# Two graph-network layers on one core: transposing the next feed-forward chunk, and the masks, without TensorE

## The chip, the cores and the metric

The kernel runs on one core of a Trainium2 chip. The metric is the device time of one execution in microseconds (us), as the median of several runs. A core has five engines that run side by side and wait for one another by semaphores: TensorE (PE; its weight load is PEld), VectorE (DVE), ScalarE (ACT), GpSimd (POOL) and SyncE (SP), which here only issues DMAs.

## The reference, cut to what matters

64 graphs of 128 nodes with 256 features each (`x`, float32) and a 128x128 adjacency matrix per graph (`adj`) go through two layers.

```
# layer 0: attention with 8 heads of 32, then a feed-forward net
normed  = layernorm(x)
q, k, v = normed @ Wq + bq, normed @ Wk + bk, normed @ Wv + bv
weights = softmax(q k^T / sqrt(32) + (2 adj - 1)) * (0.25 + 0.75 adj), rows brought to sum 1
x = x + (weights @ v) @ Wo + bo
x = x + gelu(layernorm(x) @ Wf1 + bf1) @ Wf2 + bf2       # 256 -> 1024 -> 256
# layer 1: two graph attentions, 8 heads and then 1
attn = graph_attention(layernorm(x), bias=adj, W1, ...) + x
out  = graph_attention(layernorm(attn), bias=adj, W2, ...) + attn
```

## The kernel before, in words

The graphs are worked in 16 chunks of 4 (`NC` = 16, `G` = 4), and `x_all` holds all of `x` in SBUF. Four stages run one after the other, each a loop over the 16 chunks: attention (`a_step`), feed-forward (`b_step`), first graph attention (`c1_step`), second graph attention (`c2_step`). Every engine has its own program, with functions of these names; the order within it is written out by hand, and semaphores tie them together. The diff and the prediction also count layernorms: `c = i + CB` is the one that the feed-forward stage of chunk `i` reads.

Big products are done in float32r as three matmuls, high times high, high times low, low times high. So each input exists as a high and a low part: `xh`, `xl` for the normalised input, `gh`, `gl` for the gelu's output.

A layernorm goes so: VectorE takes statistics (`stats`, L284) and aggregates them (`aggr`, L289); GpSimd computes `rstd` (`rstd_of`, L868 and L870); VectorE (L295, in the feed-forward stage) or ScalarE (L1024) writes the normalised rows `xn`; TensorE transposes them, 8 transposes of 128x128, into two PSUM banks (`ln_turn`, L1260); ScalarE copies these to `xh` (`ln_hi`, L978); VectorE subtracts to get `xl` (`ln_lo`, L301).

The feed-forward stage of chunk `i`. TensorE makes the first product in 8 slices `f` of 128 hidden features (`wide`, L1235 to L1237, 6 matmuls each, banks `f % 4`). For each slice ScalarE computes the gelu twice, to `gf` and to `gh` (L1088, L1089), and VectorE subtracts to get `gl` (L546). `gf` has two buffers: ScalarE writes that of slice `f` only when `gl` of slice `f - 2` is done. Then TensorE transposes the next chunk's `xn` (`ln_turn`), and makes the second product graph by graph, 24 matmuls each (L1461 to L1463); for every slice it waits for that slice's `gl`. VectorE adds each result to `x_all` (L579). Among its subtractions VectorE prepares the next chunk: two statistics behind subtraction 0 and two behind 1, the aggregates behind 2, the normalisation behind 4; `ln_lo` behind 7. GpSimd adds the bias to the next chunk's rows once they are normalised (`add_bias`, L849). In the chunk before the last, TensorE computes constants of the next stage behind the third graph (`setup_constants`, L1266 and L1281), which wait for the `xl` of the last chunk.

The masks. In the attention and first graph-attention stages SyncE loads a chunk's adjacency matrices to `adj_in` (two buffers) in one DMA (L768, L804). TensorE transposes them to bank `F[0]` (`adj_turn`, L1328). In attention ScalarE makes an exponential of it (`ft`, L983) and VectorE combines the two (L449); in graph attention ScalarE's exponential of it is kept in `gt_all` (L1105). The load of a later chunk is gated by these transposes.

In the attention stage TensorE also transposes the exponentials of the logits (`a_turn`, L1347), which VectorE scales (`a_pt_out`, L461). In the first graph-attention stage TensorE makes ratios (`ratios`, L1509) that VectorE scales (`c_scale`, L630).

Of the kernel before, what the change touches and what calls it, by code (L numbers as in the profile page):

```python
# [22 lines left out]
F32 = mybir.dt.float32  # L23
# [5 lines left out]
P = 128  # L29
# [25 lines left out]
def build(nc, x, adj, wq, bq, wk, bk, wv, bv, wo, bo, g1, b1, g2, b2, wf1, bf1, wf2, bf2,  # L55
# [4 lines left out]

    ctx = ExitStack()
    with ctx:
# [48 lines left out]
        REGION = 58 * 1024  # L111
# [28 lines left out]
        ft_sb = [o(f"ft{r}", [P, G, P]) for r in range(2)]  # L140
        e_sb = o("e_sb", [P, 2 * H, P])
# [22 lines left out]
        marks = o("marks", [P, 8])  # L164

# [61 lines left out]
        ln_nm = sem("ln_nm")  # L227
        adj_t = sem("adj_t")
        sp_gates = sem("sp_gates")
# [40 lines left out]

        def hb_view(par):
            return hb[par][:].rearrange("p (g h c) -> p g h c", g=G, h=H)
# [9 lines left out]
        def _(dve):  # L282
# [19 lines left out]


# [141 lines left out]

            def a_ft_out(i, par):
                dve.wait_ge(a_et, i + 1)
                f = ft_sb[par][:].rearrange("p g n -> p (g n)")
                dve.scalar_tensor_tensor(out=f, in0=F[0][:], scalar=1.0 / 3.0, in1=f, op0=ALU.add, op1=ALU.mult).then_inc(a_ft, 1)  # L449
# [42 lines left out]
            def a_step(i, half, par):  # L492
                first, tail = (isinstance(i, int) and i == n for n in (0, NC))
                for pp in range(2):
                    s, sp = i * G + (2 * pp - G), i * 2 + (pp - 2)
                    back = not (isinstance(s, int) and s < 2)
                    old = not (isinstance(s, int) and s < 3)
                    if not first:
                        a_max(sp, 0)
                    if pp == 0 and not first:  # L500
                        ln_lo(i + CA)
                    if not first:
                        a_max(sp, 1)
# [24 lines left out]
                    if pp == 0 and not tail:  # L528
                        aggr(i + CA + 1)
            chunks(dve, a_step)  # L530
# [8 lines left out]
            def b_step(i, half, par):  # L539
                final = isinstance(i, int) and i == NC - 1  # L540
                nxt = 0 if final else i + 1
                for f in range(FT):
                    if f == 2:
                        dve.wait_ge(ln_st, (i + CB + 2) * G)
# [4 lines left out]
                    if f < 2:  # L549
                        stats(i + CB + 1, nxt, 2 * f)  # L550
                        stats(i + CB + 1, nxt, 2 * f + 1)
                    if f == 2:
                        aggr(i + CB + 1)
                    if final and f == 2:
                        setup_constants()
                    if f == 4:
                        normalise(i + CB + 1, nxt)
                    if final and f == 5:
                        dve.wait_ge(b_x, 3 * G)
                        dve.wait_ge(ln_mv, (CC + 1) * G)  # L560
                        for g in range(G):
                            stats(CC + 1, 1, g)
# [193 lines left out]
        def _(sp):  # L756
# [10 lines left out]
            def load_adj(i, half, par):  # L767
                sp.dma_start(adj_in[par][:], adj[bass.ds(i * G, G)].rearrange("g p n -> p g n")).then_inc(adj_ld[par], 16)  # L768

            def load_a(i, half, par):  # L770
# [6 lines left out]
                load_adj(i, half, par)  # L777
# [9 lines left out]
            def a_step(i, half, par):  # L787
                if not (isinstance(i, int) and i == NC - 1):
                    load_a(i + 1, half + par, 1 - par)
                if par == 1 and not (isinstance(i, int) and i == 1):  # L790
# [11 lines left out]
            def load_c(i, par, first):  # L802
                gate(adj_t, i + (first - CB - 1))
                sp.dma_start(adj_in[par][:], adj[bass.ds(i * G, G)].rearrange("g p n -> p g n")).then_inc(adj_ld[par], 16)  # L804
# [5 lines left out]
            def c2_step(i, half, par):  # L810
                if not (isinstance(i, int) and i == 0):

                    gate(d_y, i * G)
                    sp.dma_start(out[bass.ds(i * G - G, G)].rearrange("g p d -> p g d"), y_sb[1 - par][:]).then_inc(y_out[1 - par], 16)
            gate(a_x, NG)
            for w, name in ((w1, "w1"), (w2, "w2")):
                sp.dma_start(stage[name][:], kp(w)).then_inc(w_l1, 16)
            for n, a in enumerate((as1, ad1, as2, ad2)):
                sp.dma_start(a_bc[n][:], a.rearrange("h k -> (h k)").partition_broadcast(P)).then_inc(w_l1, 16)
            load_c(0, 0, CC)  # L820
# [137 lines left out]
        def _(act):  # L958
# [21 lines left out]

            def a_adj(i, par):
                act.wait_ge(adj_t, i + 1)
                act.activation(ft_sb[par][:].rearrange("p g n -> p (g n)"), F[0][:], ACT.Exp,  # L983
# [97 lines left out]
            def b_step(i, half, par):  # L1081
# [8 lines left out]
                ln_hi(i + CB + 1)  # L1090
# [5 lines left out]
                if isinstance(i, int) and i == NC - 1:  # L1096
                    act.activation(warm[:], zero_g[:], ACT.Exp)
                    normalise(0, CC, range(G))
                    gt_out(0)
# [3 lines left out]
            def gt_out(i):  # L1103
                act.wait_ge(adj_t, i + NC + 1)
                act.activation(gt_all[:, bass.ds(i * W4, W4)], F[0][:], ACT.Exp).then_inc(c_gt, 1)  # L1105

            def c1_step(i, half, par):
# [7 lines left out]
                if back:  # L1115
                    gt_out(i)
# [76 lines left out]
            act.wait_ge(a_x, NG)  # L1193
            chunks(act, b_step)
# [37 lines left out]
        def _(pe):  # L1232
# [76 lines left out]
            def a_proj(i, n):  # L1309

                wait_for(pe, *(((ln_xl, (i + CA) * KT + 2)), (a_ft, i + 1), (a_qkev, i * 4 + 1), (a_qkev, i * 4 + 2))[n])
# [9 lines left out]

            def adj_turn(c, half, par, first):

                before = {CA: 0, CC: NC // 2}[first]
                pe.wait_ge(adj_ld[par], (half + 1 + before) * 16)
                pe.wait_ge(ln_xl, c * KT + 1)
                for g in range(G):
                    r = pe.transpose(F[0][:, g * P:(g + 1) * P], adj_in[par][:, g, :], ident[:])  # L1328
                r.then_inc(adj_t, 1)
# [46 lines left out]
            def a_step(i, half, par):  # L1376
                first, tail = (isinstance(i, int) and i == n for n in (0, NC))
                for pp in range(2):
# [19 lines left out]
                    if not tail:  # L1398
                        if pp == 0:
                            adj_turn(i + CA, half, par, CA)  # L1400
# [45 lines left out]
            def b_step(i, half, par):  # L1446
# [6 lines left out]
                ln_turn(i + CB + 1)  # L1453
                hi, lo = whl["wf2"]
                for g in range(G):
# [11 lines left out]
                    if isinstance(i, int) and i == NC - 1:  # L1467
                        if g == 0:
                            c_st(0, 0, 0)
                            c_st(0, 1, 0)  # L1470
                            adj_turn(CC, 0, 0, CC)
# [63 lines left out]
            def c1_step(i, half, par):  # L1535
# [11 lines left out]
                if back:  # L1547
                    adj_turn(i + CC, half, par, CC)
                    ratios(i - 1, 1 - par, 1)
                pe.wait_ge(c_gt, i + 1)  # L1550
# [125 lines left out]
```

## Time and profile before

| | |
|---|---|
| median of 3 runs | 1127.02 us (1126.33 to 1127.25) |
| the profiled execution | 1125.41 us, span 1123.6 us |
| busy TensorE, VectorE, ScalarE, GpSimd | 1070.8, 772.3, 713.8, 408.0 us |
| granted TensorE clock | 0.989 of full speed |

The span is the time from the first to the last recorded instruction; the execution takes a little more. Attention lasts to about 417 us of the span, the feed-forward stage to about 790 us, the first graph attention to about 1000 us. A row of a timeline gives the start in us, the duration in us (for a row `xN` that of N instructions together), the engine, the line, the operation, what it writes and reads, and in brackets how long the engine had been idle and for whom. The next instruction on an engine may start before the last one's recorded end.

### The profile page before, as it was taken

The page shows a single profiled execution, that of the slowest core. Times are in us where ns is not written, and L with a number is a line of the kernel's source. Part 1 is how long each engine was busy: PE and PEld are TensorE (multiplying, and loading weights), DVE is VectorE, ACT ScalarE, POOL GpSimd, SP SyncE. Part 2 cuts the span into 40 slices and gives each one's busy share as a digit, 9 for nine tenths or more (in the row PEclk, how much of TensorE's full clock was granted, in tenths as well). Part 3 has the DMA queues.
Part 4 walks back from the last instruction along what each step waited for, and adds up shares of the span by engine and source line. Part 5 has one row for each costly group of instructions (what it writes and reads, how often), then busy time and mean ns, then how long its engine had stood idle before and what let it go on. Part 6 is the DMA issues. An engine that isn't in the chain of part 4 may idle for free.

```text
span 1123.6 us, 38526 instructions
## 1 busy us (share of the span) xinstructions
PE 1070.8 (95%) x16172; PEld 945.3 (84%) x16172; DVE 772.3 (69%) x1889; ACT 713.8 (64%) x1718; POOL 408.0 (36%) x628
## 2 busy tenths in 40 slices
PE   5999999999999989999999999999999999979997
PEld 5888888888888868899889998998888888868886
DVE  4577777677776767754455445545788888859996
ACT  2777767777677755543555345536688788857774
POOL 3431121121121113332223222322387777775662
PEclk9999999999999999999999999999999999989999
DMA  7001101111100001000000000000010001002122
GB/s 225 30 30 58 32 31 31 30 31 59 30 13 2 3 27 33 1 1 1 1 1 1 1 1 1 1 1 11 11 33 22 23 23 33 3 3 73 61 76 94
DMA packets 41804, 32.10 MB, mean 29 GB/s; under 512 B 5280, under 2 KB 41376, under 8 KB 41632
## 3 DMA queue, kind: packets, MB, share of 16 engines
q1 hardware_dynamic: 37312, 29.36, 8.2%
q8 instruction: 128, 2.10, 0.8%
q10 hardware_dynamic: 4320, 0.28, 0.3%
q14 instruction: 44, 0.36, 0.1%
HBM read 21.25 MB, written 8.39 MB: 26 GB/s over the span
## 4 chain that ended last, share of the span: by engine, by line
PE 71%; POOL 11%; issue 9%; DVE 6%; ACT 2%; ACTq 1%; POOLq 0%; DVEq 0%
PE BK L1235 8%; PE BK L1237 8%; PE BK L1236 8%; PE BK L1373 6%; PE BK L1461 5%; PE BK L1462 5%; PE BK L1463 5%; PE BK L1347 5%; PE BK L1359 4%; PE BK L1340 3%; POOL x_all L938 3%; POOL x_all L849 3%; PE BK L1260 3%; POOL atc L930 2%; POOL rstd L870 1%
## 5 line engine op out<-in xcount | busy, mean ns | idle before, releaser
L1088 ACT ACTIVATE gf<-BK,bcol 128x512 f32<-128x512 f32 x128 | 88.1, 689 | 182.7 <-PE BK L1237 167.4
L868 POOL TENSOR_TENSOR ve<-mv,eps_l 128x4 f32<-128x4 f32 x64 | 15.4, 240 | 438.7 <-DVE mv L289 405.8
L1004 ACT ACTIVATE e_sb<-BK,nmx 128x128 f32<-128x128 f32 x512 | 141.5, 403 | 28.3 <-DVE nmx L455 28.3
L1461 PE MATMUL BK<-wf_hi,gh 128*128 128x256 f32 x512 | 143.5, 280 | 0.0
L1462 PE MATMUL BK<-wf_hi,gl 128*128 128x256 f32 x512 | 141.8, 277 | 0.0
L1463 PE MATMUL BK<-wf_lo,gh 128*128 128x256 f32 x512 | 141.7, 277 | 0.0
L546 DVE TENSOR_TENSOR gl<-gf,gh 128x512 fp32r<-128x512 f32 x128 | 93.4, 731 | 62.9 <-ACT gh L1089 61.1
L461 DVE TENSOR_TENSOR pt_sb<-BK,ft 128x512 f32<-128x512 f32 x128 | 85.2, 686 | 70.1 <-PE BK L1347 68.5
L1024 ACT ACTIVATE xn<-x_all,neg_mr,rstd 128x256 f32<-128x256 f32 x188 | 103.8, 611 | 5.2 <-POOL neg_mr L877 4.8
L1237 PE MATMUL BK<-xh,wf_lo 128*128 128x512 f32 x256 | 100.8, 394 | 0.0
L1236 PE MATMUL BK<-xl,wf_hi 128*128 128x512 f32 x256 | 100.6, 393 | 0.0
L1235 PE MATMUL BK<-xh,wf_hi 128*128 128x512 f32 x256 | 99.9, 390 | 0.5 <-DVE x_all L477 0.5
L579 DVE TENSOR_TENSOR x_all<-BK,x_all 128x256 f32<-128x256 f32 x64 | 27.1, 423 | 105.3 <-PE BK L1463 105.3
L455 DVE TENSOR_REDUCE nmx<-BK 128x8 f32<-128x1024 f32 x64 | 76.7, 1219 | 32.9 <-PE BK L1340 32.9
L1462 PEld LDWEIGHTS BK<-wf_hi,gl 128*128 128x128 f32 x512 | 96.3, 188 | 0.0
L1463 PEld LDWEIGHTS BK<-wf_lo,gh 128*128 128x128 f32 x512 | 96.2, 188 | 0.0
L1461 PEld LDWEIGHTS BK<-wf_hi,gh 128*128 128x128 f32 x512 | 96.1, 188 | 0.0
L284 DVE BATCH_NORM_STATS2 st<-x_all 128x6 f32<-128x256 f32 x256 | 92.1, 411 | 4.6 <-DMA x_all<-in_x_dram 4.1
L630 DVE SCALAR_TENSOR_TENSOR pp<-BK,gt_all 128x512 f32<-128x512 f32 x128 | 81.9, 682 | 16.6 <-PE BK L1509 16.6
L849 POOL TENSOR_TENSOR x_all<-x_all,bo_bc 128x256 f32<-128x256 f32 x64 | 44.6, 730 | 133.2 <-ACT xn L1024 118.6
L849 POOL TENSOR_TENSOR x_all<-x_all,c_bc 128x256 f32<-128x256 f32 x128 | 89.9, 733 | 4.0 <-ACT xn L1024 2.6
L1089 ACT ACTIVATE gh<-BK,bcol 128x512 fp32r<-128x512 f32 x128 | 87.0, 680 | 0.0
(204 smaller groups left out, 2869.7 us busy)
## 6 DMA issues: line engine op xcount, KB each, us to landing
x_all<-in_x_dram SPq DMA_DIRECT2D x16, 512.0 KB, 4.1
adj_in<-in_adj_dram SPq DMA_DIRECT2D x32, 256.0 KB, 2.9
out_dram<-y SPq DMA_DIRECT2D x16, 512.0 KB, 3.0
s_wf<-in_L_gnn_Wf_dram SPq DMA_DIRECT2D x2, 1024.0 KB, 9.9
s_w<-in_L_gnn_W_dram SPq DMA_DIRECT2D x2, 256.0 KB, 2.9
s_wq<-in_L_gnn_Wq_dram SPq DMA_DIRECT2D x1, 256.0 KB, 5.7
s_wk<-in_L_gnn_Wk_dram SPq DMA_DIRECT2D x1, 256.0 KB, 6.3
s_wv<-in_L_gnn_Wv_dram SPq DMA_DIRECT2D x1, 256.0 KB, 8.0
```

The lines of the kernel that those rows point to most:

```text
L284: dve.bn_stats(st[:, g, :], xs(i, g)).then_inc(ln_st, 1)
L546: dve.tensor_tensor(gl[:, f, :], gf[f % 2][:], gh[:, f, :].bitcast(F32), ALU.subtract).then_inc(b_gl, 1)
L849: pool.tensor_tensor(xs(i, g), xs(i, g), bias[:], ALU.add).then_inc(signal, 1)
L1004: e = act.activation(e_sb[:, j, :], LE[:, r, q, :], ACT.Exp, bias=nmx[:, j:j + 1], scale=1.0)
L1024: act.activation(xn[:, g, :], xs(nxt, g), ACT.Identity, scale=rstd[:, g:g + 1], bias=neg_mr[:, g:g + 1]).then_inc(ln_xn, 1)
L1088: act.activation(gf[f % 2][:], BK[:, f % 4, :], ACT.Gelu, bias=bcol[:, 6 + f:7 + f])
L1235: pe.matmul(dst, w_hi, m_hi, start=start, stop=False)
L1236: pe.matmul(dst, w_hi, m_lo, start=False, stop=False)
L1237: return pe.matmul(dst, w_lo, m_hi, start=False, stop=stop)
L1461: pe.matmul(dst, gh[:, f, n], hi[:, f, :], start=(f == 0), stop=False)
L1462: pe.matmul(dst, gl[:, f, n], hi[:, f, :], start=False, stop=False)
L1463: r = pe.matmul(dst, gh[:, f, n], lo[:, f, :], start=False, stop=(f == FT - 1))
```

## The change

In the feed-forward stage the next chunk's normalised rows are not transposed by TensorE any more, except in the last chunk. VectorE turns `xn` in 32x32 blocks (`block_turn`, two instructions of 128x512) into a new tile `tb_ln`. SyncE moves the blocks between partitions with 16 DMAs from `tb_ln` back into the room of `xn`. ScalarE makes `xh` from there (`turned_hi`, behind its gelus) and VectorE `xl` (`turned_lo`, now ahead of the third graph's residual addition). VectorE's preparations move: all four statistics behind subtraction 0, the aggregates behind 1, normalisation and block turn behind 3.

The masks are loaded with their blocks already in transposed places, in four DMAs a chunk of 128-byte runs, and turned by one VectorE instruction of 128x512 (`adj_tr`). In attention ScalarE and VectorE read `adj_tr`. SyncE stores it to a DRAM tensor `adj_kept`, from which the first graph-attention stage loads it in one DMA and takes the exponential without transposing. The working region of SBUF grows from 58 to 60 KB per partition.

```diff
+    adj_kept = nc.dram_tensor("adj_kept", [NC, P, G * P], F32, kind="Internal").ap()
+        adj_tr = [o(f"adj_tr{r}", [P, G * P]) for r in range(2)]
+        tb_ln = o("tb_ln", [P, 2 * KT * 2, W4 // 4])
+        turned = xn[:].rearrange("p g d -> p (g d)").rearrange("p (k a x) -> p k a x", k=KT, a=4)
+        def turned_rows(kt):
+            return turned[:, kt].rearrange("p a (g n) -> p g a n", g=G)
+        def by_graph(t):
+            return t.rearrange("p (g a n) -> p g a n", g=G, a=4)
...
VectorE
+            def block_turn(c):
+                dve.wait_ge(ln_xn, (c + 1) * G)
+                wait_for(dve, ln_ld, (c - CB - 1) * 256)
+                blocks = xn[:].rearrange("p g (b n) -> p b g n", n=32)
+                for kt in range(KT):
+                    dve.transpose(tb_ln[:, 4 * kt:4 * kt + 4, :].rearrange("p b (g n) -> p b g n", g=G),
+                                  blocks[:, 4 * kt:4 * kt + 4]).then_inc(ln_t, 1)
+            def turned_lo(c):
+                for kt in range(KT):
+                    dve.wait_ge(ln_xh, c * KT + kt + 1)
+                    dve.tensor_tensor(by_graph(xl[:, kt, :]), turned_rows(kt), by_graph(xh[:, kt, :].bitcast(F32)),
+                                      ALU.subtract).then_inc(ln_xl, 1)
+            def adj_turn(half, par):
+                dve.wait_ge(adj_ld[par], (half + 1) * 64)
+                wait_for(dve, adj_st[par], half * 16)
+                dve.transpose(adj_tr[par][:], adj_in[par][:].rearrange("p g n -> p (g n)")).then_inc(adj_t, 1)
+                    if pp == 1 and not (isinstance(i, int) and i >= NC - 1):
+                        adj_turn(half + par, 1 - par)
...
b_step of VectorE
-                    if f == 2:
+                    if f == 1:
                         dve.wait_ge(ln_st, (i + CB + 2) * G)
-                    if f < 2:
-                        stats(i + CB + 1, nxt, 2 * f)
-                        stats(i + CB + 1, nxt, 2 * f + 1)
-                    if f == 2:
+                        for g in range(G):
+                            stats(i + CB + 1, nxt, g)
+                    if f == 1:
                         aggr(i + CB + 1)
-                    if f == 4:
+                    if f == 3:
                         normalise(i + CB + 1, nxt)
+                        if not final:
+                            block_turn(i + CB + 1)
-                ln_lo(i + CB + 1)
+                if final:
+                    ln_lo(i + CB + 1)
                 for g in range(G):
+                    if g == 2 and not final:
+                        turned_lo(i + CB + 1)
...
SyncE
+                blocks = adj[bass.ds(i * G, G)].rearrange("g (r p) (c n) -> c p g r n", p=32, n=32)
+                for c in range(4):
+                    sp.dma_start(adj_in[par][c * 32:(c + 1) * 32].rearrange("p g (r n) -> p g r n", n=32),
+                                 blocks[c]).then_inc(adj_ld[par], 16)
+            def keep_adj(i, par):
+                gate(adj_t, i + 1)
+                sp.dma_start(adj_kept[bass.ds(i, 1)].rearrange("o p n -> p (o n)"), adj_tr[par][:]).then_inc(adj_st[par], 16)
+            def b_step(i, half, par):
+                if i < NC - 1:
+                    gate(ln_t, (i + CB + 2) * KT)
+                    for q in range(4):
+                        for a in range(4):
+                            sp.dma_start(turned[32 * q:32 * q + 32, :, a, :],
+                                         tb_ln[32 * a:32 * a + 32, q:8:4, :]).then_inc(ln_ld, 16)
...
ScalarE
+            def turned_hi(c):
+                act.wait_ge(ln_ld, (c - CB) * 256)
+                for kt in range(KT):
+                    act.activation(by_graph(xh[:, kt, :]), turned_rows(kt), ACT.Copy).then_inc(ln_xh, 1)
...
TensorE
-            def adj_turn(c, half, par, first):
...
-                ln_turn(i + CB + 1)
+                    ln_turn(i + CB + 1)     # in the last chunk alone
```

## Rows read from the trace of the kernel before

**Rows 1.** Busy time by stretch, the feed-forward stage: stretch, its length, each engine's busy time.
```profile
426.00:789.00 363.00, 359.72 (x2402) 327.35 (x2401) 197.12 (x475) 179.49 (x295) 97.06 (x102) 1.00 0.01 2
```

**Rows 2.** Timeline of TensorE, one feed-forward chunk, from its first product's end.
```profile
499.77 1.04 PE L1260 MATMUL BK<-ident,xn 128*128 128x128 f32 x8
500.56 0.37 PE L1461 MATMUL BK<-wf_hi,gh 128*128 128x256 f32 x1
500.76 0.28 PE L1462 MATMUL BK<-wf_hi,gl 128*128 128x256 f32 x1
```

**Rows 3.** Timeline of ScalarE, the same chunk and the next one's first gelu.
```profile
490.36 0.69 ACT L1088 ACTIVATE gf<-BK,bcol 128x512 f32<-128x512 f32 x1 [10.90 <-PE BK L1237]
...
499.97 0.69 ACT L1088 ACTIVATE gf<-BK,bcol 128x512 f32<-128x512 f32 x1
500.55 0.68 ACT L1089 ACTIVATE gh<-BK,bcol 128x512 fp32r<-128x512 f32 x1
...
513.12 0.69 ACT L1088 ACTIVATE gf<-BK,bcol 128x512 f32<-128x512 f32 x1 [10.91 <-PE BK L1237]
```

**Rows 4.** Timeline of VectorE, the same chunk.
```profile
492.27 0.74 DVE L284 BATCH_NORM_STATS2 st<-x_all 128x6 f32<-128x256 f32 x2
...
495.08 0.38 DVE L289 BATCH_NORM_AGGREGATE mv<-st 128x2 f32<-128x6 f32 x4
495.77 0.69 DVE L546 TENSOR_TENSOR gl<-gf,gh 128x512 fp32r<-128x512 f32 x1 [0.32 <-ACT gh L1089]
...
497.76 1.38 DVE L295 TENSOR_SCALAR xn<-x_all,mv,rstd 128x256 f32<-128x256 f32 x4
...
499.89 0.98 DVE L546 TENSOR_TENSOR gl<-gf,gh 128x512 fp32r<-128x512 f32 x1 [0.16 <-ACT gh L1089]
...
506.30 0.42 DVE L579 TENSOR_TENSOR x_all<-BK,x_all 128x256 f32<-128x256 f32 x1 [2.30 <-PE BK L1463]
```

**Rows 5.** Timeline of GpSimd, the same chunk.
```profile
495.81 1.53 POOL L870 TENSOR_TENSOR rstd<-ve,neg_half 128x4 f32<-128x4 f32 x1
499.22 4.10 POOL L849 TENSOR_TENSOR x_all<-x_all,bf_bc 128x256 f32<-128x256 f32 x4 [1.87 <-DVE xn L295]
```

**Rows 6.** Groups by line, VectorE: busy us, mean ns of one, then idle time.
```profile
L648 DVE TENSOR_SCALAR b_row<-b_row 128x128 f32<-128x128 f32 x16 | 5.2, 322 | 0.4 <-ACT b_row L1170 0.4
```

**Rows 7.** Timeline of ScalarE, second feed-forward chunk, its last gelu.
```profile
454.21 0.69 ACT L1088 ACTIVATE gf<-BK,bcol 128x512 f32<-128x512 f32 x1 [1.83 <-DVE gl L546]
```

**Rows 8.** Timeline of SyncE's queue, small loads ahead of the feed-forward stage.
```profile
418.77 0.43 SPq L819 DMA_DIRECT2D a_bc<-in_L_gnn_a_dst_dram  x1
419.25 0.51 SPq L819 DMA_DIRECT2D a_bc<-in_L_gnn_a_src_dram  x1
```

**Rows 9.** The mask tile's view: its loads, from issue to landing.
```profile
DMA to landing us min/median/max: 2.5/2.9/9.7
```

**Rows 10.** Groups by line, ScalarE: an instruction from SBUF to SBUF.
```profile
L1150 ACT ACTIVATE inv<-row_c,half_row 64x512 f32<-64x512 f32 x64 | 46.1, 721 | 1.2
```

**Rows 11.** Timelines of ScalarE, TensorE and VectorE, one attention chunk.
```profile
250.31 1.15 ACT L1004 ACTIVATE e_sb<-BK,nmx 128x128 f32<-128x128 f32 x4
...
251.34 0.60 PE L1328 MATMUL BK<-ident,adj_in 128*128 128x128 f32 x4
251.77 0.60 PE L1347 MATMUL BK<-ident,e_sb 128*128 128x128 f32 x4
...
269.85 1.29 DVE L461 TENSOR_TENSOR pt_sb<-BK,ft 128x512 f32<-128x512 f32 x2 [2.01 <-PE BK L1347]
```

**Rows 12.** Timelines of VectorE and TensorE, one chunk of the first graph attention.
```profile
901.57 1.28 DVE L630 SCALAR_TENSOR_TENSOR pp<-BK,gt_all 128x512 f32<-128x512 f32 x2
...
902.99 1.17 PE L1509 MATMUL BK<-row_c,inv 4*128 4x128 f32 x32
```

**Rows 13.** Timeline of TensorE, feed-forward chunk before the last: the next stage's constants.
```profile
759.18 0.95 PE L1266 MATMUL BK<-cols,wc 128*128 128x1 f32 x8
```

**Rows 14.** Timeline of VectorE, the start: the first low parts.
```profile
15.42 1.29 DVE L301 TENSOR_TENSOR xl<-BK,xh 128x512 fp32r<-128x512 f32 x2 [2.86 <-ACT xh L978]
```

More of the change, by code:

```diff
@@ L108, in build @@
         xl = sb("xl", [P, KT, W4], F32R)
-        REGION = 58 * 1024
+        REGION = 60 * 1024
         base_of_region = (nc.sbuf_base + 31) // 32 * 32
@@ L227, in build @@
         ln_nm = sem("ln_nm")
+        ln_ld = sem("ln_ld")
         adj_t = sem("adj_t")
+        adj_st = [sem("adj_st0"), sem("adj_st1")]
         sp_gates = sem("sp_gates")
@@ L448, in a_ft_out @@
                 f = ft_sb[par][:].rearrange("p g n -> p (g n)")
-                dve.scalar_tensor_tensor(out=f, in0=F[0][:], scalar=1.0 / 3.0, in1=f, op0=ALU.add, op1=ALU.mult).then_inc(a_ft, 1)
+                dve.scalar_tensor_tensor(out=f, in0=adj_tr[par][:], scalar=1.0 / 3.0, in1=f, op0=ALU.add, op1=ALU.mult).then_inc(a_ft, 1)
             def a_max(sp, half):
@@ L529, in a_step @@
                         aggr(i + CA + 1)
+            adj_turn(0, 0)
             chunks(dve, a_step)
@@ L765, in kp, with load_adj @@
                 return w.rearrange("(k p) n -> p k n", p=P)
-            def load_adj(i, half, par):
-                sp.dma_start(adj_in[par][:], adj[bass.ds(i * G, G)].rearrange("g p n -> p g n")).then_inc(adj_ld[par], 16)
+            def load_adj(i, par):
+                blocks = adj[bass.ds(i * G, G)].rearrange("g (r p) (c n) -> c p g r n", p=32, n=32)
[5 more added lines that the diff above has]
+                sp.dma_start(adj_kept[bass.ds(i, 1)].rearrange("o p n -> p (o n)"), adj_tr[par][:]).then_inc(adj_st[par], 16)
             def load_a(i, half, par):
@@ L776, in load_a @@
                 gate(adj_t, i - 1)
-                load_adj(i, half, par)
+                load_adj(i, par)
                 if isinstance(i, int) and i == 0:
@@ L789, in a_step @@
                     load_a(i + 1, half + par, 1 - par)
+                keep_adj(i, par)
                 if par == 1 and not (isinstance(i, int) and i == 1):
@@ L802, in load_c @@
             def load_c(i, par, first):
-                gate(adj_t, i + (first - CB - 1))
-                sp.dma_start(adj_in[par][:], adj[bass.ds(i * G, G)].rearrange("g p n -> p g n")).then_inc(adj_ld[par], 16)
+                gate(c_gt, i - 1)
+                sp.dma_start(adj_in[par][:].rearrange("p g n -> p (g n)"),
+                             adj_kept[bass.ds(i, 1)].rearrange("o p n -> p (o n)")).then_inc(adj_ld[par], 16)
             def c1_step(i, half, par):
@@ L814, in c2_step @@
                     sp.dma_start(out[bass.ds(i * G - G, G)].rearrange("g p d -> p g d"), y_sb[1 - par][:]).then_inc(y_out[1 - par], 16)
+            for r in range(2):
+                gate(adj_st[r], NC // 2 * 16)
             gate(a_x, NG)
@@ L819, in _ @@
                 sp.dma_start(a_bc[n][:], a.rearrange("h k -> (h k)").partition_broadcast(P)).then_inc(w_l1, 16)
+            def b_step(i, half, par):
[5 more added lines that the diff above has]
+                                         tb_ln[32 * a:32 * a + 32, q:8:4, :]).then_inc(ln_ld, 16)
+            chunks(sp, b_step)
             load_c(0, 0, CC)
@@ L1089, in b_step @@
                     act.activation(gh[:, f, :], BK[:, f % 4, :], ACT.Gelu, bias=bcol[:, 6 + f:7 + f]).then_inc(b_gh, 1)
-                ln_hi(i + CB + 1)
+                if i == NC - 1:
+                    ln_hi(i + CB + 1)
+                else:
+                    turned_hi(i + CB + 1)
                 if isinstance(i, int) and i == 0:
@@ L1098, in b_step, with gt_out @@
                     normalise(0, CC, range(G))
-                    gt_out(0)
+                    gt_out(0, 0, 0)
                     far_minima(0)
                     row_exps(0)
-            def gt_out(i):
-                act.wait_ge(adj_t, i + NC + 1)
-                act.activation(gt_all[:, bass.ds(i * W4, W4)], F[0][:], ACT.Exp).then_inc(c_gt, 1)
+            def gt_out(i, half, par):
+                act.wait_ge(adj_ld[par], NC // 2 * 64 + (half + 1) * 16)
+                act.activation(gt_all[:, bass.ds(i * W4, W4)], adj_in[par][:].rearrange("p g n -> p (g n)"), ACT.Exp).then_inc(c_gt, 1)
             def c1_step(i, half, par):
@@ L1115, in c1_step @@
                 if back:
-                    gt_out(i)
+                    gt_out(i, half, par)
                     row_exps(i)
@@ L1193, in _ @@
             act.wait_ge(a_x, NG)
+            for r in range(2):
+                act.wait_ge(adj_st[r], NC // 2 * 16)
             chunks(act, b_step)
@@ L1320, in a_vproj @@
                     r.then_inc(a_v, 1)
-            def adj_turn(c, half, par, first):
[L1324 to L1329, printed above, removed]
             def a_logits(sp, i, par, pp):
@@ L1399, in a_step @@
                         if pp == 0:
-                            adj_turn(i + CA, half, par, CA)
                             if first:
```

7 lines of the change are left out of this document (2 added, 5 removed).

## The prediction, written before the result was known

> **What bounds the kernel now.** I read in this order. First the busy time by stretch: in the feed-forward stretch TensorE is busy 359.72 of 363.00 us, VectorE and ScalarE about half of it [rows 1]. Then one feed-forward chunk on every engine. ScalarE's first gelu of a chunk starts every 513.12 - 490.36 = 22.76 us, after 10.91 us of waiting for TensorE [rows 3]; so that stage is TensorE's, and has 16 chunks. Then who could be late there: the gelus of the eight slices of a chunk come at (499.97 - 490.36) / 7 = 1.373 us, back to back, and each slice needs VectorE's `gl` subtraction before TensorE can use it [rows 3, 4]. `gf` has two buffers, so gelu 6 may start only when subtraction 4 is done, gelu 7 when subtraction 5 is. That wait is seen once in an ordinary ScalarE row: 1.83 us, in the second chunk, and that chunk is among the longest [rows 7]. Last the attention and first graph-attention chunks, for the mask transposes.
>
> **The change, part by part.**
>
> *Feed-forward, what goes.* Eight TensorE transposes a chunk: the next work starts 500.56 - 499.77 = 0.79 us after them [rows 2], and the first matmul behind them takes 0.09 more than the rest, so 0.88 (500.76 - 500.56 = 0.20 against the 0.113 below). 15 chunks lose them (the last keeps them): 13.2 us if nothing else is late.
>
> *Feed-forward, what VectorE gets.* It normalises one slice earlier (behind subtraction 3) and then makes two block turns of 128x512 ahead of subtraction 4. I replay the traced chunk. Four row statistics behind subtraction 0, from 492.27, at (0.74 for two) end at 493.7; subtraction 1 to 494.4; the aggregates 0.38 to 494.8, instead of 495.45 [rows 4]. GpSimd's rstd ended at 495.81 + 1.53 = 497.34, 1.9 us behind the aggregates [rows 5]; so now 496.7. Subtraction 3 starts at 495.77 as before and is done by then. The normalisation takes 1.38: 498.1. The trace has no block turn. Bounds: below, 0.32 us, the row of a 128x128 single-source instruction; above, four times that, 1.29 (no gain from the longer row) [rows 6]. I take 0.61, at which a 128x512 subtraction lets the next one start (0.69 long) [rows 4], since column count is what such rows go by. Two turns: 499.4; subtraction 4 done at 500.1, where before it was done ahead of 498.6, the old start of gelu 6 (499.97 - 1.37). Gelu 6 is thus 1.55 late, gelu 7 starts at 501.5, its second half ends 1.26 later (as 500.55 + 0.68 stands to 499.97 [rows 3]) at 502.8, subtraction 7 at 503.5.
>
> *What TensorE makes of it.* A graph's 24 matmuls take 0.42 + 2.30 = 2.72 us [rows 4], 0.113 each. Without transposes it starts the second product at 499.77 and wants slice 7 after 21 of them, at 502.15. It waits 1.37 us. The chunk is 22.76 - 0.88 + 1.37 = 23.25: what the transposes gave is lost, and 0.49 more. Before, TensorE wanted slice 7 about 503.0 and had it at 502.0: the transposes were the cover of that second.
>
> GpSimd's bias additions start when the normalisation ends and run 4.1 us [rows 5]; beside them one subtraction took 0.98 instead of 0.69 [rows 4]. That subtraction had slack; now the turns and subtractions 4 and 5 lie there, and I add 0.3: 23.55.
>
> *The moves.* 16 DMAs a chunk from the sync engine's queue. Two that follow each other start 0.48 us apart, and a DMA issue takes 0.43 to 0.51 [rows 8]; 15 x 0.51 puts the last at 499.6 + 7.7 = 507.3. Mask loads land 2.5 us or more after issue [rows 9], though of eight times the size; I take 2 to 2.9. Then two ScalarE copies from SBUF instead of PSUM, up to 0.72 each [rows 10], and VectorE's second low part, 0.7: ready between 511.4 and 512.3. TensorE with the wait above is through the chunk at 499.77 + 1.37 + 4 x 2.72 = 512.0, with the 0.3 at 512.3. The two meet, so the transfers hide only just; each 0.1 us more on an issue is 1.5 us a chunk on this side. The Vector queue stands at this wait ahead of the third residual addition, which TensorE needs only in the next chunk. Nothing else is on the sync queue in this stage but the weight loads at its start. I take +0.8 a chunk for the first 14: 11.2.
>
> *The chunk before the last.* The constants of the next stage (from 759.18 [rows 13]) stand behind its third graph and wait for the low parts of the next chunk. These came early; now they come at about 22.9 into the chunk, while TensorE is at 2.72 before its end. It waits some 2.1, plus the 0.8: +2.9.
>
> *Attention.* Four mask transposes leave TensorE, 251.77 - 251.34 = 0.43 us a chunk [rows 11]. The transposes behind them need the exponentials, done at 250.31 + 1.15 = 251.46; so 0.3 is given back, 0.43 at most, none at least: -0.3 x 15 = -4.5. VectorE's block turn (0.6) falls ahead of its wait of 2.01 us for TensorE [rows 11], which covers it; were it gone, it would be 0.6 x 15 = 9. Stores and the loads in 128-byte runs are a chunk ahead of use.
>
> *Start.* The mask load becomes four DMAs, three more issues of 0.5 ahead of the first weights. VectorE sits 2.86 us for ScalarE's copy behind those weights [rows 14], so most of it is covered; the extra small packets on queues that are full here also hold ScalarE's own column loads. Bounds 0 and 4; I take +1.5.
>
> *First graph attention.* Four transposes a chunk go. The ratio matmuls behind them start at 902.99, when VectorE's scaling, on which they wait, ended at 901.57 + 1.28 = 902.85 [rows 12]. So the transposes lay beside VectorE: 0.1 x 15 = -1.5, at most 0.43 x 15 = -6.5, at least 0.
>
> **Sum.** +11.2 + 2.9 - 4.5 + 1.5 - 1.5 = +9.6 on the profiled execution's 1125.41 (span 1123.6, 1.8 around it), which lies 1.6 under the median 1127.02: 1135.0 and 1136.6.
>
> **The Trainium skill on the turn.** By VectorE: DVE Perf Modes, The three transpose paths, a block turn of 128x128 two-byte elements takes 311 ns and TensorE's whole transpose 390, and its rules for kernel authors send a 128x128 transpose to TensorE where PSUM is a fit place for it. No row here has a block turn; the 0.32 row of the same shape agrees with the 311. The trace has TensorE at 0.1 us a transpose in a run of eight, well under that page, so the rule speaks against the change more strongly than its own figures. DMA: Bandwidth & Descriptors, Rules for kernel authors, says that under 64 KB one pays mostly overhead; these DMAs carry 32 KB. By it the queue, and not the bytes, is the price, as the 0.5 us rows say.
>
> **Rivals.**
> 1. *TensorE simply gets shorter.* Gelu 6 doesn't wait, since the turn and the normalisation fit into VectorE's idle time (it idles between subtractions). For: VectorE is busy half the chunk. Against: the replay, and the 1.83 us wait under a late normalisation. It gives -13.2 - 4.5 + 1.5 - 1.5 + 2 for the constants = -15.7: 1111. Chance 0.14.
> 2. *The gain and the wait cancel.* A turn takes 0.32, the lower bound: gelu 6 is 0.58 less late and no contention, the chunk is 22.7, and the constants still cost 2.1. About -1 + 2.1 - 4.5 + 1.5 - 1.5 = -3: 1124; with a half of the contention 1127. Chance 0.13.
> 3. *The turns or the transfers are dear.* A turn takes 1.29: 2 x 0.68 more, the chunk 24.6 to 24.9; or an issue takes 0.6 and more, and the low parts come at 513.5 or later. Speaks for it: queue and TensorE meet already. +2 x 14 + 3 - 4.5 = +26: 1153. It decides from a turn of 0.9 us or an issue of 0.6. Chance 0.2.
> 4. *The forecast*, 1136.6: chance 0.53, its own range 1129 to 1145.
>
> **How the numbers follow.** This kernel's measurement tells 0.2%, 2.3 us, from no change. Slower: the forecast, rival 3: 0.73. Same: two thirds of rival 2: 0.09. Faster: rival 1 and the rest: 0.18. The range takes in the forecast's own, rival 3's price and half of rival 2: 1123 to 1156.
>
> **What would show it.** In the profile after: ScalarE's first gelu comes every 23.3 to 23.9 us; ScalarE waits about 1.5 us for `gl` before the seventh gelu of each chunk; TensorE waits for `gl` in the first graph of the second product. The block turn has 0.6 to 0.75 us; the 16 issues span 7.7 us; the last lands near 509.6 on the traced chunk's clock, and if TensorE's wait stands ahead of the first product instead, the transfers are what binds. TensorE waits near 2 us ahead of the constants once. Attention chunks are 0.3 shorter, graph-attention chunks nearly the same. I am wrong if the feed-forward chunk is 22.4 or less, or if the gelus keep 1.37 us.

## The result, and the profile after

The changed kernel takes 1158.41 us (median of 4 runs, 1154.4 to 1161.31) against 1127.13 for the kernel before: ratio 1.0265, interval 1.0237 to 1.0293. The forecast was 1136.6 us, with a range of 1123 to 1156. The direction was right, the size was three times too small: +9.6 us forecast, +31.3 measured.

I cut both traces at the last residual addition of a stage. Attention ends at 412.3 us instead of 417.0 (-4.7); the feed-forward stage takes 409.5 us instead of 375.7 (+33.8); the rest takes 334.6 instead of 330.9. That last difference can't be put down to the change by these traces: ten kernels here run the same program in the last stages (the changed one and runs 3 to 11), and their profiled executions take 330.9 to 340.5 us for it. Run 1, with the mask part alone, is lower in its median by just what its attention stage gains.

So the loss lies in the feed-forward chunks. ScalarE's timeline shows both of its waits there (start, us, engine, line, operation, tiles; in brackets the idle time before it and who ended it). After:

```profile
515.53 0.69 ACT L1156 ACTIVATE gf<-BK,bcol 128x512 f32<-128x512 f32 x1 [2.57 <-PE BK L1310]
...
522.99 0.68 ACT L1157 ACTIVATE gh<-BK,bcol 128x512 fp32r<-128x512 f32 x1
525.17 0.69 ACT L1156 ACTIVATE gf<-BK,bcol 128x512 f32<-128x512 f32 x1 [1.51 <-PE BK L1310]
...
537.11 1.15 ACT L1047 ACTIVATE xh<-xn 128x512 fp32r<-128x512 f32 x2 [9.52 <-DMA xn<-tb_ln]
540.83 0.69 ACT L1156 ACTIVATE gf<-BK,bcol 128x512 f32<-128x512 f32 x1 [2.57 <-PE BK L1310]
```

The second row with a wait is the seventh gelu, behind 1.51 us of idle time; in [rows 3] the idle time between gelus is 0.1, so it is 1.40 us late. The label names TensorE, which had long been done (the slice is one of those that came every 1.37 us), so it is VectorE's `gl`, which frees `gf`. [rows 3] have no such wait. The chunk is 540.83 - 515.53 = 25.30 us instead of 22.76; over the twelve chunks from 466.32 to 763.57 it is 24.77 on average, between 24.08 and 25.46. VectorE, where [rows 4] stood, and TensorE's first product:

```profile
521.63 1.39 DVE L310 TENSOR_SCALAR xn<-x_all,mv,rstd 128x256 f32<-128x256 f32 x4
523.05 1.31 DVE L325 STREAM_TRANSPOSE tb_ln<-xn 128x512 f32<-128x512 f32 x2
524.28 1.95 DVE L585 TENSOR_TENSOR gl<-gf,gh 128x512 fp32r<-128x512 f32 x2
```
```profile
513.83 0.51 PE L1308 MATMUL BK<-xh,wf_hi 128*128 128x512 f32 x1 [1.75 <-DVE xl L331]
...
527.42 0.39 PE L1524 MATMUL BK<-wf_hi,gh 128*128 128x256 f32 x1 [0.25 <-DVE gl L585]
...
528.38 0.39 PE L1524 MATMUL BK<-wf_hi,gh 128*128 128x256 f32 x1 [0.33 <-DVE gl L585]
...
539.13 0.51 PE L1308 MATMUL BK<-xh,wf_hi 128*128 128x512 f32 x1 [1.64 <-DVE xl L331]
```

TensorE idles little for `gl`, and 1.75 and 1.64 us for `xl` ahead of these two chunks (0.76 to 1.82 in the other ordinary ones). By the prediction's own last part that means: the transfers bind. The chain of waits between the two shows how (start, us, what), and SyncE's timeline has the sixteen issues as one row:

```profile
523.05 1.32 DVE tb_ln L325 x2
524.40 0.05 issue
524.45 0.59 SPq L880
525.03 0.04 issue
525.07 0.60 SPq L880
...
532.74 0.61 SPq L880
533.35 0.04 issue
533.39 1.78 SPq L880
535.17 0.04 issue
535.21 1.88 DMA xn<-tb_ln
...
537.11 0.64 ACT xh L1047
...
537.78 0.56 DVE xl L331
...
538.38 0.70 DVE xl L331
...
539.13 0.51 PE BK L1308
```
```profile
524.45 11.37 SPq L880 DMA_DIRECT2D xn<-tb_ln  x16
```

One issue every 0.64 us (the pitch), sixteen in a row. The row of 1.78 us is the fifteenth, 1.2 us longer than the others. The sixteenth starts at 535.21 and is not a row of its own: the chain counts it in the 1.88 us from issue to landing. Then come ScalarE's and VectorE's copies, and TensorE. The sixteen span 11.37 us here and 10.2 where none of them is long; 15 x 0.51 and one issue, 8.2, were forecast.

The irregular delays account for the spread of the chunks. Of the twelve ordinary ones three have none and take 24.08 to 24.13 us. Six have one issue of 1.50 to 1.97 us among the last six, one has an issue of 0.99, one a pause of 0.33 between two issues, and in one the last transfer lands 0.97 us later; each of these nine chunks is longer by about its delay. What causes the delays no run shows. Last, the chunk before the last, TensorE and the clock beside it (stretch, length, each engine's busy time, the seventh figure TensorE's clock):

```profile
786.06 1.84 PE L1339 MATMUL BK<-cols,wc 128*128 128x1 f32 x8 [3.58 <-DVE xl L331]
787.75 3.76 PE L1354 MATMUL BK<-s_w,lb_wide 128*128 128x256 f32 x8
```
```profile
787.00:789.00 2.00, 2.00 (x8) 1.82 (x8) 0.00 (x0) 0.00 (x0) 0.00 (x0) 0.50 0.00 0
789.00:791.00 2.00, 2.00 (x7) 1.55 (x6) 0.00 (x0) 0.00 (x0) 0.00 (x0) 0.50 0.00 0
```

After 3.58 us of waiting, the stage constants run with a granted clock of 0.50, the 1.2 GHz level, and take twice as long as in [rows 13]; the clock stays at that level for some 7 us in all. That chunk is 32.66 us instead of 25.51.

### The profile page after: what moved, and what is told of

It is laid out like the page before. It is cut to its first block, busy times and chain, and to the rows that moved or that the text cites. A ratio compares the mean times of both kernels' runs of the same rounds, so it can differ in the third digit from the quotient of the medians.

```text
span 1156.5 us, 38408 instructions
## 1 busy us (share of the span) xinstructions
PE 1067.2 (92%) x15924; PEld 929.3 (80%) x15924; DVE 806.2 (70%) x1935; ACT 713.9 (62%) x1718; POOL 399.7 (35%) x628
## 4 chain that ended last, share of the span: by engine, by line
PE 42%; DVE 14%; POOL 13%; SPq 12%; issue 12%; ACT 3%; DMA 3%; POOLq 0%; DVEq 0%; ACTq 0%
SPq L880 11%; PE BK L1437 6%; PE BK L1411 5%; PE BK L1423 4%; PE BK L1308 4%; PE BK L1310 3%; PE BK L1309 3%; PE BK L1404 3%; POOL x_all L1001 3%; POOL x_all L912 3%; POOL rstd L933 3%; DMA xn<-tb_ln 2%; POOL atc L993 2%; DVE gl L585 2%; DVE xn L310 2%
## 5 line engine op out<-in xcount | busy, mean ns | idle before, releaser
L931 POOL TENSOR_TENSOR ve<-mv,eps_l 128x4 f32<-128x4 f32 x64 | 20.9, 326 | 483.3 <-DVE mv L304 450.7
L1524 PE MATMUL BK<-wf_hi,gh 128*128 128x256 f32 x512 | 147.4, 288 | 10.8 <-DVE gl L585 10.8
L585 DVE TENSOR_TENSOR gl<-gf,gh 128x512 fp32r<-128x512 f32 x128 | 99.4, 786 | 52.8 <-ACT gh L1157 52.2
L1047 ACT ACTIVATE xh<-xn 128x512 fp32r<-128x512 f32 x30 | 17.3, 623 | 133.1 <-DMA xn<-tb_ln 133.1
```

The costliest lines, as they stand in the source:

```text
L585: dve.tensor_tensor(gl[:, f, :], gf[f % 2][:], gh[:, f, :].bitcast(F32), ALU.subtract).then_inc(b_gl, 1)
L1524: pe.matmul(dst, gh[:, f, n], hi[:, f, :], start=(f == 0), stop=False)
```

## The experiments

All times are medians, the ratio is to the kernel before on the same chip. "Period" is the distance of first gelus in the twelve ordinary feed-forward chunks (all but the first two, the one before the last and the last), in the profiled execution.

| run | us | ratio (interval) | period, us |
|---|---|---|---|
| before | 1127.1 | 1 | 22.76 |
| after | 1158.4 | 1.0265 (1.0237 to 1.0293) | 24.08 to 25.46 |
| 1 masks alone | 1122.45 | 0.9962 (0.9946 to 0.9978) | 22.76 |
| 2 feed-forward alone | 1163.82 | 1.0336 (1.0312 to 1.0360) | 24.09 to 26.27 |
| 3 eight transfers | 1130.42 | 1.0032 (1.0013 to 1.0052) | 23.04, some 23.37 |
| 4 through device memory | 1133.07 | 1.0063 (1.0041 to 1.0086) | 23.04 or 23.37 |
| 5 two queues | 1130.81 | 1.0042 (1.0026 to 1.0058) | 23.04 |
| 6 two queues, turns apart | 1114.09 | 0.9889 (0.9872 to 0.9905) | 21.89, two of 22.2 |
| 7 device memory, turns apart | 1119.19 | 0.9949 (0.9930 to 0.9969) | 21.89, some 22.1 to 22.8 |
| 8 as 3, narrow turns | 1124.01 | 0.9978 (0.9952 to 1.0004) | 22.54, some 22.87 |
| 9 half the bytes | 1155.75 | 1.0261 (1.0214 to 1.0308) | 23.82 to 25.04 |
| 10 one queue, turns apart | 1190.41 | 1.0550 (1.0510 to 1.0590) | 26.07 to 28.22 |
| 11 as 6, constants earlier | 1112.51 | 0.9863 (0.9827 to 0.9899) | 21.89, some 22.3 |

**1 and 2: the parts apart.** Run 1 has the mask edits only, run 2 the feed-forward edits only.

```diff
 run 1 keeps, run 2 leaves out:
+                dve.transpose(adj_tr[par][:], adj_in[par][:].rearrange("p g n -> p (g n)")).then_inc(adj_t, 1)
 run 2 keeps, run 1 leaves out:
+                        normalise(i + CB + 1, nxt)
+                        if not final:
+                            block_turn(i + CB + 1)
```


> The mask part alone (block loads, VectorE's turn, the kept copy in DRAM), the feed-forward stage as before. Theory 'issues': the masks only help; attention 4.7 us shorter as in the changed kernel, graph attention within 1 us of before, so about 1121.5 us. Rival 'masks cost later': the 3.7 us that the changed kernel's graph-attention stages are longer come from the masks' new path; then about 1126 us.

> The feed-forward part alone, masks as before. Theory 'issues': the whole loss lies here, 1127 + 34 = 1161 us, and up to 1165 us if the longer graph attention comes with it (a lower granted clock there). Rival 'masks cost later': 1157 us or less, graph-attention stages as long as before.

The masks give -0.4%, which is 4.4 us, and the feed-forward stage starts 4.4 us earlier; that stage takes as long as before, and the mean period of the first graph attention is 12.65 us in both. The feed-forward part alone costs 3.4%: its stage takes 414.2 us instead of 375.7. The two add up to the changed kernel: 0.9962 x 1.0336 = 1.0297, against 1.0265, a difference that the three intervals together don't resolve. In run 2 one more thing is seen. In three ordinary chunks the clock falls to half behind TensorE's wait for `xl`, after waits of 1.77, 2.02 and 1.81 us:

```profile
494.14 0.50 PE L1283 MATMUL BK<-xh,wf_hi 128*128 128x512 f32 x1 [1.77 <-DVE xl L328]
```
```profile
495.00:497.00 2.00, 2.00 (x7) 1.57 (x6) 0.00 (x0) 0.85 (x2) 0.00 (x0) 0.58 0.00 0
```

In the changed kernel's ordinary chunks it stays at 1.00 after waits of up to 1.82 us.

**3: half the transfers.** Eight of the 16 DMAs, half of the blocks not moved. (In this run and in 4 and 8 the counts that the engines wait for are adapted too; those lines are left out.)

```diff
-                        for a in range(4):
+                        for a in range(2):
                             sp.dma_start(turned[32 * q:32 * q + 32, :, a, :],
```


> Only 8 of the 16 DMAs of a feed-forward chunk are issued (half of the blocks are not moved); all else as in the changed kernel. Theory 'issues' (16 issues of 0.64 us in a row set the chunk): the low parts come 8 x 0.64 = 5.1 us earlier, the queue is hidden, and the gelu wait bounds the chunk at 23.3 to 23.5 us instead of 24.1 to 25.3; the wait ahead of the constants and the half clock behind it go. About 1138 us. Rival 'gelus alone' (the late gelus and the contention of the transfers make the loss, the queue is hidden anyway): within 3 us of 1158 us.

28 of the 31 us go, some 8 more than I expected. TensorE no longer waits ahead of the chunk; the seventh gelu is late as before, and the period is 23.04: the price that late gelus have by themselves, +0.28 on 22.76. (Why some chunks of runs 3 and 4 take 23.37 I haven't traced.)

**4: fewer issues, more bytes.** One store of the turned tile to device memory and four loads back: five issues and twice the bytes.

```diff
+                    sp.dma_start(tb_kept, tb_ln[:].rearrange("p b x -> p (b x)")).then_inc(ln_sv, 16)
+                    gate(ln_sv, (i + 1) * 16)
+                    kept = tb_kept.rearrange("(a p) (k q x) -> q p k a x", a=4, k=KT, q=4)
                     for q in range(4):
-                        for a in range(4):
-                            sp.dma_start(turned[32 * q:32 * q + 32, :, a, :],
-                                         tb_ln[32 * a:32 * a + 32, q:8:4, :]).then_inc(ln_ld, 16)
+                        sp.dma_start(turned[32 * q:32 * q + 32], kept[q]).then_inc(ln_ld, 16)
```


> The blocks go by one DMA to DRAM and back by four (5 issues a chunk instead of 16, the same bytes twice). Theory 'issues': store 0.6 to issue and 3.0 to land, four loads of 0.64, the last landing 2.5 us later: ready 8 us behind the turn instead of 12.4, so hidden; the chunk 23.3 to 23.5 us, about 1138 us. Rival 'bytes and latency of a transfer': two trips and twice the bytes, so not faster than 1158 us.

The whole result is computed here, through a slower kind of path (the store lands in 2.6 us and then a load in 3.0, against 1.9 for a direct transfer), and 25 us go all the same. The store carries the whole tile of 512 KB and occupies the queue for 0.33 us, a load of 128 KB to 32 partitions for 0.61.

**5: sixteen transfers on two queues.**

```diff
-                    for q in range(4):
+                    for q in range(2):
...
+                    act.wait_ge(ln_t, (i + CB + 2) * KT)
+                    for q in range(2, 4):
+                        for a in range(4):
+                            act.dma_start(turned[32 * q:32 * q + 32, :, a, :],
+                                          tb_ln[32 * a:32 * a + 32, q:8:4, :]).then_inc(ln_ld, 16)
                     turned_hi(i + CB + 1)
```


> Both parts of the change; the 16 transfers are the same, but eight are issued on SP's queue and eight by ScalarE on its own queue, after its eighth gelu. My theory (the chain of 16 issues at 0.64 us on one engine sets the changed chunk): SP's eight span 5.1 us from 524.4 in the numbers of the changed kernel's chunk, ScalarE's eight run from 525.3 to about 530.5 and land 1.9 us later, at about 532.4; so TensorE waits at the start of a chunk no longer, and the late gelus are left: periods of 23.04 to 23.4 as with half the moves, 1127 to 1134 us. Rival (the transfers themselves, 16 of 32 KB with short rows, are what takes the time, not their issue): the same transfers still end at about 535 and the period stays near 24.5, 1155 us or more.

The same 16 transfers, the same bytes, and a period of 23.03 to 23.07 us, that of run 3. ScalarE's queue, in its timeline:

```profile
545.72 0.69 ACT L1156 ACTIVATE gf<-BK,bcol 128x512 f32<-128x512 f32 x1
545.77 0.59 ACTq L1164 DMA_DIRECT2D xn<-tb_ln  x1
546.30 0.69 ACT L1157 ACTIVATE gh<-BK,bcol 128x512 fp32r<-128x512 f32 x1
546.39 5.63 ACTq L1164 DMA_DIRECT2D xn<-tb_ln  x7
...
553.31 1.16 ACT L1047 ACTIVATE xh<-xn 128x512 fp32r<-128x512 f32 x2 [6.32 <-DMA xn<-tb_ln]
```

**9: sixteen issues, half the bytes.** The counterpart of run 5. Each DMA also has half as many rows of 512 bytes.

```diff
-                            sp.dma_start(turned[32 * q:32 * q + 32, :, a, :],
-                                         tb_ln[32 * a:32 * a + 32, q:8:4, :]).then_inc(ln_ld, 16)
+                            sp.dma_start(turned[32 * q:32 * q + 32, 0, a, :],
+                                         tb_ln[32 * a:32 * a + 32, q, :]).then_inc(ln_ld, 16)
```


> The changed kernel with all its 16 transfers a chunk on SP's queue, each cut to half its columns (16 KB instead of 32 KB); the other half of the turned data isn't moved. My theory (the number of issues on one queue sets the chunk, not the bytes): the pitch stays near 0.64 us, the period at 24.2 to 24.6 us, the kernel at 1150 to 1158 us. Rival (the issue takes as long as it does because of what it moves, by its descriptors or bytes): the pitch falls towards 0.3 to 0.4 us, the period to the 23.04 of the kernel with eight transfers, 1128 to 1134 us.

Hardly anything moves: 1155.75 us, and the chain has nearly the same pitch and even the same kind of long issue:

```profile
523.48 0.51 SPq L880
523.99 0.04 issue
524.03 0.59 SPq L880
...
532.26 1.59 SPq L880
...
533.90 1.78 DMA xn<-tb_ln
...
535.70 0.64 ACT xh L1047
```

Sixteen issues without a long one span 10.0 us instead of 10.2, and the landing takes 1.8 instead of 1.9; the shortest chunk is 23.82 us instead of 24.08.

Runs 3, 4, 5 and 9 agree: what sets the changed chunk is how many DMAs one queue issues between the turn and the next chunk.

**8: the turn made small.** Eight transfers as in run 3, and each block turn cut to 32 of 512 columns; the rest of the turned data isn't computed.

```diff
-                    dve.transpose(tb_ln[:, 4 * kt:4 * kt + 4, :].rearrange("p b (g n) -> p b g n", g=G),
-                                  blocks[:, 4 * kt:4 * kt + 4]).then_inc(ln_t, 1)
+                    dve.transpose(tb_ln[:, 4 * kt, 0:32], blocks[:, 4 * kt, 0]).then_inc(ln_t, 1)
```


> Half the moves (eight of the 16 transfers) as before, and each of the two block turns cut to 32 of its 512 columns, so that VectorE has about 1.2 us less ahead of gl of slice 5; the rest of the turned data isn't computed. Theory of the late gelus: period from 23.04 to about 22.0 to 22.3 us, 1113 to 1121 us against 1130 with whole turns. Rival (something else holds the chunk of the half-move kernel at 23.04, such as what the missing transposes leave TensorE's order in): no change, 1128 to 1132.

The right sign and about half of the size: the gelu is still late.

```profile
538.98 1.39 DVE L310 TENSOR_SCALAR xn<-x_all,mv,rstd 128x256 f32<-128x256 f32 x4
540.46 0.31 DVE L326 STREAM_TRANSPOSE tb_ln<-xn 128x32 f32<-128x32 f32 x2
540.69 2.20 DVE L585 TENSOR_TENSOR gl<-gf,gh 128x512 fp32r<-128x512 f32 x2
```
```profile
541.83 0.69 ACT L1157 ACTIVATE gf<-BK,bcol 128x512 f32<-128x512 f32 x1 [0.81 <-DVE gl L585]
```

0.81 us of idle time instead of 1.51, period 22.54 instead of 23.04. Here the label names the true releaser. The turns are 1.0 us shorter and the gelu comes 0.70 earlier; the subtractions behind them, beside which GpSimd's bias additions run, took 2.20 us as a pair, 0.25 more than in the changed kernel. I expected the gelu on time and didn't allow for those. Why they are slow stays open: GpSimd's additions alone are not enough, since in run 6 subtractions beside the same additions take 0.65 us each (below).

**6 and 7: the turns apart.** One block turn behind subtraction 4, the other behind subtraction 5; only the normalisation stays ahead of subtraction 4. Run 6 on the two queues of run 5, run 7 on the way of run 4.

```diff
                     if f == 3:
                         normalise(i + CB + 1, nxt)
-                        if not final:
-                            block_turn(i + CB + 1)
+                    if f in (4, 5) and not final:
+                        block_turn(i + CB + 1, f - 4)
```


> As the kernel with the issues on two queues, and the two block turns of VectorE are taken apart: one behind gl of slice 5, one behind gl of slice 6, instead of both behind the normalisation ahead of slice 5. My theory (with the issues out of the way the 1.5 us wait of the seventh gelu for gl sets the chunk): gl of slice 5 ends 1.3 us earlier, the seventh gelu starts on time, and TensorE runs through the chunk; the last gl comes at about the time at which the second product asks for it. The period falls to 21.9 to 22.2 us, below the 22.76 of the kernel before; with 15 chunks x -0.7 and the masks' -4.5 the kernel takes 1112 to 1120 us. Rival (the order of VectorE's work only moves the wait to a later gl): the period stays at 23.0 and the time at 1127 to 1134.

> The five-issue way through device memory (one store, four loads) with the two block turns taken apart in the same way. Same theory: period 21.9 to 22.2 us and 1112 to 1120 us, from 1133 with both turns together. Rival: 1130 to 1135, the period stays at 23.04 or 23.37.

Period 21.89 us in both: 22.76 less the 0.88 of the transposes is 21.88. That is the gain of rival 1, reached. VectorE's timeline of run 6 has the turns where it was idle before:

```profile
534.14 1.39 DVE L310 TENSOR_SCALAR xn<-x_all,mv,rstd 128x256 f32<-128x256 f32 x4
535.44 0.69 DVE L584 TENSOR_TENSOR gl<-gf,gh 128x512 fp32r<-128x512 f32 x1
536.04 0.71 DVE L324 STREAM_TRANSPOSE tb_ln<-xn 128x512 f32<-128x512 f32 x1
536.67 0.65 DVE L584 TENSOR_TENSOR gl<-gf,gh 128x512 fp32r<-128x512 f32 x1
537.24 0.70 DVE L324 STREAM_TRANSPOSE tb_ln<-xn 128x512 f32<-128x512 f32 x1
537.87 0.65 DVE L584 TENSOR_TENSOR gl<-gf,gh 128x512 fp32r<-128x512 f32 x1
```

Run 6 beats the kernel before by 1.1%, run 7 by 0.5%. In run 7 TensorE waits 3.35 us ahead of the constants, in run 6 1.03, and the chunk with them takes 31.45 us in run 7 and 27.45 in run 6.

**10: the turns apart, one queue.** The edit of run 6, with all sixteen issues left on the sync engine's queue.

> The changed kernel with the two block turns taken apart (behind gl of slices 5 and 6), all 16 issues still on SP's queue. My theory (of the two limits the issue chain is the outer one): the gelus come on time, but the second turn ends about 1.0 us later in the chunk, so the chain of issues starts and ends 1.0 us later: periods of 25.2 to 25.6 us, 1165 to 1174 us, slower than the changed kernel's 1158 although its gelus don't wait. Rival (the late gelus cost time of their own beside the issues): 1145 to 1155.

Slower, as the theory says, and by more than it says: period 26 to 28 us. The gelus don't wait for `gl`. The chain starts 10.0 to 11.5 us into the chunk instead of 8.9: 1.0 by the edit, as expected, the rest because TensorE's first slices come slower. TensorE waits 2.5 to 4.1 us ahead of every chunk but the first, and with thirteen of these fourteen waits its clock falls to half. In the chunk shown it waited 4.07 us, and its first matmuls are 0.43 us from one to the next instead of 0.23. Its granted clock (seventh figure):

```profile
519.00:521.00 2.00, 0.41 (x1) 0.41 (x2) 1.76 (x4) 0.73 (x2) 0.00 (x0) 0.89 0.00 0
521.00:523.00 2.00, 2.00 (x6) 1.52 (x6) 0.20 (x1) 0.00 (x0) 0.00 (x0) 0.50 0.00 0
523.00:525.00 2.00, 2.00 (x8) 1.61 (x7) 0.14 (x1) 1.27 (x2) 0.00 (x0) 0.75 0.00 0
```

The same edit thus gains 1.5% with the issues out of the way (run 5 to 6) and loses 2.8% with them in it.

**11: the constants.** TensorE's constants step waits for the last reader of its banks, the first chunk's low parts, instead of the last chunk's.

```diff
-                pe.wait_ge(ln_xl, (NC - 1 + CB) * KT + 2)
+                pe.wait_ge(ln_xl, CB * KT + 2)
```


> As the kernel with two queues and the turns taken apart, and TensorE's step of constants in the chunk before last waits for the xl of the first chunk, the last that reads the PSUM banks it writes, instead of that of the last chunk. Theory: the 1.03 us wait ahead of those products goes, and with it most of the stretch of some 4 us at half clock behind it; that chunk falls from 27.45 to about 24.5 to 25 us, the kernel to 1110 to 1113 us. Rival (the small products themselves lower the clock, as TensorE's wait does not): only the 1.0 us goes, 1113 us, with the clock at half level behind them all the same.

```profile
742.95 0.95 PE L1343 MATMUL BK<-cols,wc 128*128 128x1 f32 x8
743.75 1.97 PE L1358 MATMUL BK<-s_w,lb_wide 128*128 128x256 f32 x8
```

No wait, and the durations of [rows 13]; in run 6 the second step took 2.85 us, behind a wait of 1.03 ahead of the first. That chunk falls from 27.45 to 24.95 us. The kernel's time, 0.9863 against 0.9889, isn't told apart from run 6 by the intervals. Its median is the lowest here, 1.4% under the kernel before.

## Why the prediction was wrong, step by step

- *Transposes gone, -0.88 a chunk.* Right (runs 6, 7 and 11).
- *Block turn 0.61.* Measured 0.69 long, the next starting 0.63 behind (runs 6 and after). Right.
- *Gelu 6 late by 1.55, for `gl`.* Measured 1.40 (1.51 idle); the next one came 1.15 us behind it, not 1.37. *TensorE's wait for it, 1.37.* In run 3 the first and last matmuls of the second product start 1.15 us further apart than in run 6, where no gelu is late. *The chunk it leaves, 23.25 to 23.55.* Measured 23.04 where nothing else binds (runs 3 and 5). The mechanism was right; the term was 0.2 to 0.5 too dear.
- *Sixteen issues at 0.51, the transfers "hide only just".* **This is the step that failed.** The issues measured 0.64 from start to start, not the 0.51 taken from [rows 8], which were other DMAs. That is 15 x 0.13 = 1.95 us a chunk, and it makes the shortest chunks 24.08; with the forecast's pitch the chain would have allowed about 22.1 (an estimate, 24.08 - 1.95) and stayed hidden behind the gelus' 23.04. On top came the irregular delays, an issue of 1.5 to 2.0 us in six of the 15 chunks and smaller ones in three, which make the mean of 24.77; nothing in the prediction allowed for them. I had written that each 0.1 us is 1.5 us a chunk, and that an issue of 0.6 decides for rival 3; [rows 8] allowed no such confidence in their upper end, and an issue to 32 partitions at another offset had no row at all. Rival 3, 1153 us at a chance of 0.2, is what came, by its half on the issues; the turns were not dear. The landing, 1.88 us from the start of the last issue, was just under the 2 to 2.9 forecast; ScalarE's copies (0.62 each, up to 0.72 forecast) and VectorE's (0.70) were as forecast. In sum: ordinary chunks 24.77 instead of 23.55, 12 x 1.22 = 14.6 us over the forecast; the first two chunks another 1.9.
- *Chunk before the last, +2.9.* Measured 32.66 - 25.51 = +7.15. The wait was forecast at 2.9 us and was 3.58; not forecast was that TensorE would fall to the half clock behind it, for some 7 us. Without a wait (run 11) that step has no such cost.
- *Attention -4.5, start +1.5.* Measured -4.65 together, -3.0 forecast; 23.86 to 23.67 a chunk is -0.19, not -0.3, and by the fourth chunk the changed kernel is already 2.8 us ahead: `xl` of the first chunk starts at 14.29 instead of 15.42 [rows 14]. So no cost of the extra issues is seen, and why the start got shorter I haven't tested.
- *First graph attention -1.5.* Nothing: 12.65 us in both (run 1). That fits transposes that lay wholly beside VectorE's work.
- *The Trainium skill.* By DMA: Bandwidth & Descriptors, Rules for kernel authors, a transfer under 64 KB pays mostly overhead. Run 9 agrees: with 16 KB an issue took 0.59 us, with 32 KB 0.60. What decided was a cost per DMA on one queue.

## What to carry to other kernels

Where many small DMAs stand in a row between a producer and a consumer, count them and multiply by the pitch of that very kind of DMA itself. If the nearest row is of another kind, put the upper bound well above it, and where the chain has no margin, forecast with that bound. Spread them over two queues, or go through device memory with fewer ones. And a stage with two limits shows only the outer one: test an inner repair with the outer limit removed, since by itself it may look like a loss (run 10 against run 6).

## What the runs showed of the hardware

- A DMA from 32 partitions to 32 others occupies the sync queue for 0.60 us, 0.64 from one to the next, with 32 KB; with 16 KB it is 0.59 and 0.63 (run 9). One store of a whole 512 KB tile to device memory takes the queue 0.33 us (run 4). ScalarE's queue shows 0.65 from one issue to the next, with one of about 0.9 near the start in most chunks of run 5, and it issues beside its own engine's running gelu.
- In six of 15 chunks of the changed kernel one issue took 1.5 to 2.0 us, and in a seventh 0.99. What that is stays open.
- After a wait of 3.58 us ahead of the constants TensorE worked at the 1.2 GHz level for some 7 us (clock 0.50). With thirteen of the fourteen waits of 2.5 to 4.1 us between run 10's chunks it did for 3 to 4 us; with the one of 3.11 us ahead of the third chunk it didn't. After waits of up to 1.82 us in the changed kernel's ordinary chunks it didn't, but in run 2 it did, again for 3 to 4 us, after waits of 1.77, 1.81 and 2.02. So waits of about 1.8 us and of about 3.1 us stand on both sides: the length of a wait alone doesn't tell.
- In the constants step a wait of 1.03 us with matmuls of one column behind it had the same effect (clock 0.50 for 3 to 4 us in run 6), and without the wait the same matmuls kept the full clock (run 11).
